# Other orders of work around an attention and feed-forward kernel: maxima ahead of latents, gates among rows, inputs loaded and squared sooner, casts by pairs

## The reference

```python
c_kv, c_q = x @ w_dkv, x @ w_dq                       # ranks 64 and 192
k = concat([rope(x @ w_kr), c_kv @ w_uk])             # the rotary key is shared by the heads
q = concat([rope(c_q @ w_qr), c_q @ w_uq]);  v = c_kv @ w_uv
attn = softmax(q k^T / sqrt(192));  x = layernorm(x + (attn v) @ w_o)
g = silu(x @ w1q^T) * (x @ w3q^T);  x = layernorm(x + g @ w2q^T)
```

## Time and profile before

| | us |
|---|---|
| three runs | 928.97, 929.67, 929.88 (median 929.67) |
| profiled execution | 925.24 |
| its span | 923.4 |
| PE busy | 869.9 (94%) |
| ACT busy | 692.4 (75%) |
| DVE busy | 665.6 (72%) |
| POOL busy | 618.9 (67%) |
| DMA queue q1, share of 16 engines | 75.6% |

### The profile page before, as it was taken

The page is one execution under the profiler, slowest core; times in us unless marked ns, Lnnn a source line. Parts: engine busy times, 40 slices in busy tenths (PEclk is TensorE's granted clock), DMA queues, the critical chain, the costliest instruction groups (busy, mean ns, idle before and its releaser), DMA issues. The chain is left out here.

```text
span 923.4 us, 16915 instructions
## 1 busy us (share of the span) xinstructions
PE 869.9 (94%) x5128; PEld 499.6 (54%) x5128; DVE 665.6 (72%) x1055; ACT 692.4 (75%) x1113; POOL 618.9 (67%) x436
## 2 busy tenths in 40 slices
PE   8999689999999999989889969999999999998985
PEld 5668344444444444468666724444444444446874
DVE  2779678878788788844566957787878888783455
ACT  3744799999999999951353489999999999994142
POOL 0328777888788887851344766888888887885134
PEclk9899999999999999999999979999999999999998
DMA  9856799998998898980502679999899889898001
GB/s 253 251 197 139 154 205 189 177 183 161 176 190 165 159 194 170 171 193 31 200 23 55 140 153 197 188 173 183 161 175 186 166 160 197 168 168 213 5 1 46
DMA packets 423932, 145.82 MB, mean 158 GB/s; under 512 B 408188, under 2 KB 416208, under 8 KB 423120
## 3 DMA queue, kind: packets, MB, share of 16 engines
q1 hardware_dynamic: 423152, 142.91, 75.6%
q0 software_dynamic: 576, 2.10, 0.6%
q10 hardware_dynamic: 160, 0.26, 0.1%
HBM read 23.85 MB, written 7.60 MB: 34 GB/s over the span
## 5 line engine op out<-in xcount | busy, mean ns | idle before, releaser
L464 POOL TENSOR_TENSOR P_parts<-probs,P_parts 128x768 f16<-128x768 f32 x256 | 420.1, 1646 | 113.9 <-ACT P_parts L521 113.6
L521 ACT ACTIVATE P_parts<-probs 128x768 f16<-128x768 f32 x256 | 215.5, 842 | 11.0 <-DMA PT_dma<-P_parts 1.8
L896 DVE TENSOR_REDUCE small<-OO 128x1 f32<-128x1024 f32 x96 | 117.2, 1221 | 25.0 <-PE OO L1207 25.0
L1207 PE MATMUL OO<-K_hi,Q_parts 128*128 128x512 f16 x384 | 116.9, 386 | 16.9 <-DVE Q_parts L873 9.9
L1236 PE MATMUL Tb<-PT_dma,V_hi 128*64 128x512 f16 x768 | 132.3, 385 | 0.0
L906 DVE TENSOR_TENSOR PT_lo<-Ta,PT_hi 128x512 f16<-128x512 f32 x128 | 88.4, 690 | 59.9 <-ACT PT_hi L521 59.8
L896 DVE TENSOR_REDUCE small<-Sa 128x1 f32<-128x1024 f32 x96 | 116.9, 1218 | 19.0 <-PE Sa L1207 19.0
L628 ACT ACTIVATE probs<-OO,small,scales 128x1024 f32<-128x1024 f32 x96 | 115.1, 1199 | 10.3 <-DVE small L899 10.3
L1207 PE MATMUL Sa<-K_hi,Q_parts 128*128 128x512 f16 x384 | 117.3, 388 | 4.5 <-ACT probs L628 3.2
L628 ACT ACTIVATE probs<-Sa,small,scales 128x1024 f32<-128x1024 f32 x96 | 115.5, 1203 | 4.9 <-issue 3.8
L896 DVE TENSOR_REDUCE small<-Sb 128x1 f32<-128x1024 f32 x64 | 77.9, 1218 | 17.3 <-PE Sb L1207 17.3
(11 more groups left out here) (299 smaller groups left out, 1550.0 us busy)
## 6 DMA issues: line engine op xcount, KB each, us to landing
Q_parts<-turned_parts SPq DMA_DIRECT2D x64, 128.0 KB, 2.4
TT<-ternary SPq DMA_DIRECT2D x2, 2304.0 KB, 8.8
Q_parts<-Q_parts SPq DMA_DIRECT2D x16, 256.0 KB, 3.0
PT_dma<-P_parts SPq DMA_TRANSPOSE x256, 3.9
ternary<-tern SPq DMA_DIRECT2D x1, 2304.0 KB, 10.1
wo<-in_L_attn_w_o_dram SPq DMA_DIRECT2D x4, 512.0 KB, 8.4
xq<-in_L_attn_x_dram SPq DMA_DIRECT2D x2, 1024.0 KB, 13.4
wq_low<-Wq_lo SPq DMA_DIRECT2D x1, 2048.0 KB, 14.5
```

What stands on the lines that cost most here:

```text
L464: nc.gpsimd.tensor_tensor(P_parts[:, n % DEEP, 1, :], probs[n % DEEP][:, KP * P:S], P_parts[:, n % DEEP, 0, :], ALU.subtract).then_inc(par ...
L521: return nc.scalar.activation(o, i, ACT.Copy, scale=scale)
L896: nc.vector.tensor_reduce(nmax[:, n % 4:n % 4 + 1], scores_bank(n)[:, :], AX.X, ALU.max, negate=True).then_inc(row_max, 1)
L1207: last = mm(bank[:, m * HALF:(m + 1) * HALF], Q_parts[:, p * 2 + a, part, q:q + P], c[:, m * HALF:(m + 1) * HALF], start=(k == 0), stop=(k ...
```

## The change

- ScalarE, inner pairs: the cast of an odd tile is made together with that of the next even one, behind the even tile's exponential. First and last pair keep their order but for the seam.
- VectorE: the maximum of a batch's tile 0 stands right behind the last `rotate`, ahead of the latents. The last group's two rotary casts move from ScalarE to VectorE, into iterations 0 and 2 of the first pair; GpSimd's rests and SyncE's moves of them are one tile later. ScalarE runs one small exponential (`exp_warm`) behind group 2 of the queries.
- Tail: the first gate is made before the fourth late attention row, the first norm of the second half after the third gate; a fifth hidden product stands before the second turn; the first half's down products begin before the second half's hidden products; results use the banks in another turn; `result_rows_1` is split into two pairs with powers, norms and stores of their own; tile 5 of the gate comes last in the late down products.
- Next batch: x and small weights are loaded before the low query weights; squares come ahead of two gate casts; the bound's row is transposed before the third hidden product of the second half, in bank `SQ[2]` in place of `Ta`.

```diff
-        Y_BANKS = (SQ[2], SQ[3], SQ[2], SQ[3], SQ[2], SQ[3], Ta[:, :], Tb[:, :])
+        Y_BANKS = (SQ[2], SQ[3], Ta[:, :], Tb[:, :]) * 2
...
                 if b:
+                    sp.wait_ge(att_ps, b * QT)
+                    sp.wait_ge(att_res, (b - 1) * 48 + 24)
+                    sp.dma_start(Wq_lo[:, :, :, :].rearrange("p h c m -> p (h c m)").bitcast(F), wq_low).then_inc(wq_in, 16)
                     sp.wait_ge(wq_in, 16)
...
-                        if first and n in (4, 6):
+                        if first and n in (5, 7):
                             rotary_moves(GROUPS - 1, n // 2 - 2)
...
-                if b + 1 < B:
-                    sp.wait_ge(att_ps, (b + 1) * QT)
-                    sp.wait_ge(att_res, b * 48 + 24)
-                    sp.dma_start(Wq_lo[:, :, :, :].rearrange("p h c m -> p (h c m)").bitcast(F), wq_low).then_inc(wq_in, 16)
...
-                        if first and n in (1, 3):
-                            rotary_parts_low(GROUPS - 1, n // 2)
+                        if first and n in (2, 4):
+                            rotary_parts_low(GROUPS - 1, n // 2 - 1)
...
-                power(1, b * 4 + 4)
-                store(1)
+                power(slice(4, 6), 4)
+                power(slice(6, 8), 5)
+                store(1, 0)
+                store(1, 1)
...
                         for j in range(2):
                             rotary_parts_high(g, j)
+                    if g == GROUPS - 2:
+                        nc.scalar.activation(exp_warm, cq_up, ACT.Exp, scale=0.0)
...
                     for n in range(0, TILES, 2):
                         ahead = not (last and n == TILES - 2)
+                        before = not first and not (last and n > 0)
+                        behind = first and n < TILES - 2 or last
                         if ahead:
                             exponent(t0 + n + 2, n + 2)
-                            part_high(t0 + n + 2, n + 2, ...)
+                            if before:
+                                cast(n + 1)
+                            cast(n + 2)
                             exponent(t0 + n + 3, n + 3)
                         transposed_high(t0 + n + 1, n + 1)
-                        if ahead:
-                            part_high(t0 + n + 3, n + 3, ...)
-                        if first and n == 0:
-                            rotary_parts_high(GROUPS - 1, 1)
+                        if ahead and behind:
+                            cast(n + 3)
 
                 part_high(b * PAIRS * TILES, 0, None)
                 exponent(b * PAIRS * TILES + 1, 1)
                 part_high(b * PAIRS * TILES + 1, 1, None)
-                rotary_parts_high(GROUPS - 1, 0)
...
                 x1_high(0)
-                for t in range(HT):
+                silu(0, 0)
+                silu(0, 1)
+                gate_high(0, 0)
+                gate_high(0, 1)
+                for t in range(2, HT):
                     silu(0, t)
                     gate_high(0, t)
-                    if t == 3:
+                    if t == 4:
                         x1_high(1)
                 silu(1, 0)
                 silu(1, 1)
+                if b + 1 < B:
+                    squares(b + 1)
                 gate_high(1, 0)
                 gate_high(1, 1)
-                if b + 1 < B:
-                    squares(b + 1)
...
+                for g in range(GROUPS):
+                    rotate(g)
+                    if g == GROUPS - 1:
+                        maximum(b * PAIRS * TILES, 0)
+                    latents_low(g, 0)
+                    if g:
+                        rotary_parts_low(g - 1)
+                    latents_low(g, 1)
+
+                def rotary_parts_high(g, j):
+                    dve.wait_ge(rope_sum, b * 2 * GROUPS + 2 * g + j + 1)
+                    dve.wait_ge(turned_out[j], b * 64 * GROUPS + 64 * g)
+                    nc.vector.tensor_copy(turned_parts[:, j, 0, :], turned[:, j, :]).then_inc(rope_hi, 1)
...
                             if not (last and m >= TILES):
                                 maximum(t0 + m, m)
+                        if first and n in (0, 2):
+                            rotary_parts_high(GROUPS - 1, n // 2)
                         transposed_low(pair * (TILES // 2) + n // 2, n + 1)
...
-                maximum(b * PAIRS * TILES, 0)
-                latents_low(GROUPS - 1, 1)
...
                 x1_low(0)
-                attention_rows(1)
+                for t in range(4, 7):
+                    attention_row(t)
                 gate_tile(0, 0)
-                first_norm(1)
+                attention_row(7)
+                add_eps(slice(4, 8), A0 + 24)
                 gate_tile(0, 1)
                 gate_tile(0, 2)
+                first_norm(1)
                 gate_tile(0, 3)
+                gate_tile(0, 4)
                 x1_low(1)
-                for t in range(4, HT):
+                for t in range(5, HT):
                     gate_tile(0, t)
                 gate_tile(1, 0)
                 gate_tile(1, 1)
-                result_rows_0()
+                result_rows_0(0)
                 if b + 1 < B:
                     input_norm(b + 1)
+                result_rows_0(2)
+                add_eps(slice(0, 4), A0 + 36)
...
-                result_rows_1()
+                result_pair(4, A0 + 36)
+                result_pair(6, A0 + 42)
                 dve.sem_inc(y_read, 1)
-                second_norm(1)
+                second_norm(range(4, 6), 4)
+                second_norm(range(6, 8), 5)
...
                 hidden(0, 3)
+                hidden(0, 4)
                 turn_x1(1)
-                for t in range(4, HT):
+                for t in range(5, HT):
                     hidden(0, t)
+                down((0, 1), range(3), True)
                 pe.wait_ge(x1T_lod, b * 4 + 4)
                 hidden(1, 0)
                 hidden(1, 1)
-                down((0, 1), range(HT), True)
+                down((0, 1), range(3, HT), True)
                 down((2, 3), range(HT), False)
+                if b + 1 < B:
+                    input_row(b + 1)
                 for t in range(2, HT):
                     hidden(1, t)
-                    if b + 1 < B and t == 2:
-                        input_row(b + 1)
...
-                down((4, 5, 6, 7), range(HT), True)
+                down((4, 5), range(HT - 1), True)
+                down((6, 7), range(HT - 2), False)
+                down((4, 5), range(HT - 1, HT), True)
+                down((6, 7), range(HT - 2, HT), False)
```

More of the change, by code:

```diff
@@ L107, in build @@
         x_sums, ffs = halves[:, 0:8], halves[:, 8:16]
+        exp_warm = small[:, 8:9]
         minus_half, nmax = small[:, 0:4], small[:, 4:8]
@@ L496, in low_part, with store @@
                                             ALU.subtract).then_inc(glo_done, 1)
-                def store(h):
-                    pool.wait_ge(y_ready, b * 2 + h + 1 + Y0)
-                    nc.gpsimd.dma_start(out_v[b][:, 4 * h:4 * h + 4, :], yo[h]).then_inc(y_out, 16)
+                def store(h, part=0):
+                    pool.wait_ge(y_ready, b * 3 + Y0 + (1 if h == 0 else part + 2))
+                    rows = slice(2 * part if h else 0, 2 * part + 2 if h else 4)
+                    nc.gpsimd.dma_start(out_v[b][:, 4 * h + rows.start:4 * h + rows.stop, :], yo[h][:, rows, :]).then_inc(y_out, 16)
                 for t in range(HT):
@@ L795, in input_bound @@
             def input_bound(b):
-                bank = (Sa, Ta)[b]
+                bank = (Sa, SQ[2])[b]
                 dve.wait_ge(x_row, b + 1)
@@ L986, in _ @@
                 dve.wait_ge(xr_in, b * 64 + 64)
-                attention_rows(0)
+                for t in range(4):
+                    attention_row(t)
+                add_eps(slice(0, 4), A0 + 12)
                 first_norm(0)
@@ L1009, in result_row, with result_rows_0 @@
                                                    tok(x1, t), ALU.mult, ALU.add).then_inc(att_res, 1)
-                def result_rows_0():
-                    for t in range(4):
+                def result_rows_0(first_row):
+                    for t in range(first_row, first_row + 2):
                         n = A0 + 24 + 3 * t
@@ L1057, in _ @@
                 gate_tile(1, 3)
-                second_norm(0)
+                second_norm(range(4), 3)
                 if b + 1 < B:
@@ L1161, in input_row @@
                     pe.wait_ge(x_max, batch + 1)
[L1162 removed]
+                    if batch:
+                        pe.wait_ge(att_res, (batch - 1) * 48 + 25)
+                    nc.tensor.transpose((Sa, SQ[2])[batch][0:1, 0:P], x_most, ident[:, :]).then_inc(x_row, 1)
                 def bound_sums(batch):
[L1165 removed]
+                    bank = (Sa, SQ[2])[batch]
                     pe.wait_ge(ones_ready, 1)
@@ L1389, in down @@
                         for u in tiles:
-                            if i == 0 and u < 6:
```

(5 more changed lines are left out.)

74 lines of the change are left out of this document (31 added, 43 removed).

## The result

| | before | after |
|---|---|---|
| median of the timed runs, us | 929.32 | 912.37 (911.15 to 914.08) |
| profiled execution, us | 925.24 | 911.15 |
| its span, us | 923.4 | 909.3 |

What follows compares the result with a forecast made beforehand. TensorE was taken as the bound, with ScalarE hardly behind. Terms 5.6 + 5.5 + 3.3 + 4.5 + 1.6 = 20.5 us off the runs' median of 929.67 gave 909.2 us, range 904.5 to 918.5.

Steps and rivals of the forecast that it cites:

- Inner pairs, 5.6 us: Inner pairs: casts by pairs remove TensorE's 0.47 us wait per pair, in 6 pairs of 2 batches; bounds 0 and 6.0.
- (1): Rival, inner pairs: no gain, the 0.47 us per pair comes back at another tile; 914.8 us, chance 0.14.
- (4): Rival, slower: transposing DMAs of the bunched tiles land late, costing 25.2 us; 934.4 us, chance 0.05.
- Third scores: Batch starts: with the maximum ahead, third scores come 2.6 us sooner in batch 0 and 3.4 in batch 1.
- Exponential 12, 3.3 and 5.5 us: Batch starts: exp(12) comes this much sooner in batches 0 and 1, 1.9 us each from rotary casts off ScalarE.
- rival (2): Starts give half (table-load drain, a clock that falls anyway, rotary moves in the queue); 913.6 us, chance 0.12.
- rival (3): Starts: the DMA queue doesn't hold back the bunched casts (no 1.9 and 1.2 us); 906 us, chance 0.06.
- The clock of the starts: Start of batch 1: TensorE's wait falls to 2.5 us and the clock stays up, gaining 0.4 and 1.8 us.
- Casts on VectorE: Batch starts: two rotary casts moved there take 1 us each in its gaps, between 0.68 and ScalarE's 1.05 plus standing.
- Tail of batch 0, 4.5 us: Inputs' turn at 474.5 instead of 479.05, as TensorE's waits for input bound, gates and banks shrink; bounds 1 and 6.3.
- rival (5): The tail of batch 0 gives 1.5 us instead of 4.5; 912.2 us, chance 0.08.
- Tail of batch 1, 1.6 us: TensorE ends 1.4 us sooner and the last store is issued at 917.75 instead of 919.31; bounds 0 and 2.5.

Runs made afterwards that it cites:

- early_prefetch: The changed kernel with all four prefetches issued ahead of the second pair, in place of ahead of pairs 1, 2, 4 and 6; ratio 0.995.
- max_old: The changed kernel with the maximum of tile 0 behind the latents again; 921.05 us, ratio 0.9919.
- casts_on_act: The changed kernel with the last group's two rotary casts back on ScalarE, their moves and residuals one tile sooner; ratio 0.9827.
- wait_moved: The changed kernel with SyncE's wait for the last latents' move put ahead of the last group's first rotary move; 909.73 us, ratio 0.982.
- old_loads: The changed kernel with the low query weights loaded first again and the next inputs behind them; ratio 0.9818.
- pairs_only: The kernel before with only the casts by pairs in the inner pairs; ratio 0.9982.
- starts_only: The kernel before with only the changed starts (maximum ahead, warming exponential, rotary casts on VectorE, later moves and residuals); ratio 0.9971.
- spread_fill: spread with values products put ahead of the last transposes in each batch's last pair; 904.77 us, ratio 0.974.
- low_on_dve: spread_fill with the last group's second rotary residual on VectorE in place of GpSimd; 902.7 us, ratio 0.9728.
- spread: wait_moved with the last group's eight rotary moves issued one or two at a time; 908.45 us, ratio 0.9784.

## Why the prediction was right, and where its terms were not

- **Inner pairs, 5.6 us.** Mechanism right: 37.26 us per pair, gap gone, landings unchanged, so rivals (1) and (4) are out. In the changed kernel's profile the six pairs are 1.8 and 2.9 us shorter, 4.7 in all. The missing 0.9 are the groups behind a prefetch, which early_prefetch shows: the term took one steady pair for all six. The whole column "pairs" gains 4.0; the other 0.7 is lost around the ends of the six.
- **Third scores.** They were forecast 2.6 and 3.4 us sooner and measured 2.8 and 3.4 us sooner. max_old shows that the maximum's place alone makes this.
- **Exponential 12, 3.3 and 5.5 us.** Measured 2.0 and 4.0: rival (2) in part. The step of the prediction that failed is "ScalarE, busy throughout the first pair, sets the pace. It loses two rotary casts": 1.9 us each, of which casts_on_act finds 0.4 and 0.7 (net of the moves' place), hardly more than what repeats. ScalarE was not busy throughout; it waited for DMAs, and the casts lay in these waits. The DMA waits were there, so rival (3) is out, and sized well (2.1 and 1.9 forecast, 2.8 and 2.4 measured as the sum in each start), but the one of 2.05 us at tile 4 of batch 0 was not seen: the prediction followed the moves of the last group and not the wait for the latents' landing ahead of them. wait_moved puts the waits of batch 0 where the prediction had them and gains only 0.3 us.
- **The clock of the starts.** Behind the third scores batch 1 runs at 1.00, as forecast, where it had 0.62. But "I take the clock to stay up" held only so far: behind the wait of 2.81 us at tile 7 it is 0.83 from 540 to 550. In batch 0 it fell to 0.66 behind the 4.58 us wait. No step foresaw these two. The kernel before has two falls in the start of batch 1 (0.62 behind the third scores, 0.66 from 550 to 560), the changed kernel one.
- **Casts on VectorE.** Taken at 1 us each. The two rows are 0.68 and 1.41 us: right in the mean. The short one starts 0.11 us before an operation of GpSimd, which then takes 2.07 us instead of 1.64; the long one starts while GpSimd is 0.8 us into such an operation. Batch 1 has the same pair, 0.68 and 1.42.

```profile
107.63 0.68 DVE L918 CAST turned_parts<-turned 128x1024 f16<-128x1024 f32 x1
...
112.63 1.41 DVE L918 CAST turned_parts<-turned 128x1024 f16<-128x1024 f32 x1
```

- **Tail of batch 0, 4.5 us.** Measured 4.0 (39.50 instead of 43.47; the column "tail 0" is 41.82 to 41.89 in all eleven profiles with the changed tail); rival (5) is out. The wait on the input bound is 0.5 us, not 0; one of 1.1 us for the last gate residuals came back. "The squares start at 456.1 instead of 463.1, as inputs are loaded from 423 on" has the wrong cause: the squares do start at 455.0, but old_loads gets the same without the load.
- **Tail of batch 1, 1.6 us.** Undersized: 2.4 us to the last store's issue (43.77 instead of 46.18 us behind the first hidden product) and 3.1 to the end. TensorE ends 1.75 us sooner (38.76 instead of 40.51; 1.4 forecast). The last store holds half the rows, and from its issue to the end of the span 3.4 us pass instead of 4.1: that piece was in no term, and that the smaller store is its cause is not shown. I did not try one store instead of two.

Against the columns of the table the terms missed by -1.6 (pairs), -1.3 and -1.5 (starts), -0.6 and +1.5 us (tails): together the 3.5 us between 20.5 and 17.0.

## What to carry to other kernels

When an engine is called busy throughout, list its waits first: work taken from it is worth only what doesn't lie in them. When a queue is shared, follow every wait in it, also those ahead of the first use, and expect a removed wait to come up again at the next shared resource. Moving one short operation on the path (a maximum) was worth more than all moves that relieved an engine.

## What the runs showed of the hardware

At the end of each batch's last pair TensorE waits 2.35 us ahead of the last transposes in twelve of the fourteen kernels, so in 24 places. In 14 of them the 3.4 us that follow have a granted clock of 1.00 and the first hidden product comes 31.5 us later. In the other 10 the clock is 0.50 to 0.71 (0.50 is the lower level, 1.2 GHz, all the time) and the product comes 32.9 to 33.1 us later. The work and the wait are the same. These are such 3.4 us of batch 0, in pairs_only first, then in the changed kernel:

```profile
404.24:407.64 3.40, 3.40 (x16) 1.58 (x16) 0.69 (x1) 0.60 (x1) 2.22 (x2) 0.53 0.83 160
```
```profile
403.39:406.79 3.40, 3.40 (x28) 2.41 (x29) 1.44 (x2) 0.60 (x1) 2.61 (x3) 1.00 0.82 159
```

So a wait of this length costs itself and then, some of the time, 1.5 us more; what decides it is not shown. This is where pairs_only lost its gain in batch 0. Such falls also go with the spread of one kernel's times: of the twelve runs of starts_only the fastest (919.34 us) has a mean granted clock of 0.988 and the slowest (931.34) one of 0.975. By estimate that is 24 us more at half the speed, or 12 us of work lost, the whole difference. In the four places of spread_fill and low_on_dve, where 1.05 us or so is waited, the clock stays at 1.00; four are few, but the direction is the forecast one.

The landing of a transposing DMA is 3.7 to 4.1 us in the steady groups and longer in places. With eight large loads right ahead in the queue it was 6.7 us; with the two of one prefetch 4.7 (changed kernel, issued at 146.50 and at 185.26) and 6.3 (kernel before, at 582.01). Small moves show no rule: with two ahead it was 5.5 us in spread and 4.0 in low_on_dve, with four ahead 3.8 in the changed kernel. Between 137 and 141 us of the changed kernel it reached 5.8 us with neither right ahead. What else lengthens it is not shown.
